# Reading attention scores two slots at a time, splitting the next stage's context from slot 6, and normalising rows on ScalarE in a fused decoder kernel

## The reference

```python
# first attention of layer 0: sign weights, 32 heads of 16, 8 key/value heads
q = x_n @ sign(Wq).T * scale_q     # k, v likewise; scale = mean |w| per output row
attn = softmax(q @ k.T / 4)        # per head, 64 x 64 scores
x = x + (attn @ v) @ sign(Wo).T * scale_o
# then: cross-attention with heads of 128, RMS-normed q and k; sparse feed-forward
# layer 1: attention with ALiBi and causal mask, cross-attention with key mask,
#          mixture of experts with a gate over 8 experts
```

## Time and profile before

| | |
|---|---|
| median of 3 runs | 2214.14 us (2213.44 to 2216.16) |
| the profiled execution's own time | 2213.81 us |
| its span, first to last instruction | 2212.0 us |
| mean granted TensorE clock | 0.99 of full |
| TensorE busy | 2118.3 us, 96% |
| VectorE, ScalarE, GpSimd busy | 61%, 46%, 41% |
| DMA | 82 MB, mean 37 GB/s |

### The profile page before, as it was taken

The page is one execution under the profiler, slowest core; times in us unless marked ns, Lnnn a source line. Parts: engine busy times, 40 slices in busy tenths (PEclk is TensorE's granted clock), DMA queues, the critical chain, the costliest instruction groups (busy, mean ns, idle before and its releaser), DMA issues. The chain is left out here.

```text
span 2212.0 us, 45005 instructions
## 1 busy us (share of the span) xinstructions
PE 2118.3 (96%) x18686; PEld 1718.5 (78%) x18686; DVE 1344.8 (61%) x2350; ACT 1028.0 (46%) x1754; POOL 902.6 (41%) x675
## 2 busy tenths in 40 slices
PE   6997999999999999999999999999998899999998
PEld 5665888888887888888888877888887677777766
DVE  6985544443334453444433558797785788888856
ACT  5774553545535455354543552111102667667632
POOL 2787241432414414143241345122122668778611
PEclk9998999999999999999999999999999899999999
DMA  4000111110112101111010123000002100100002
GB/s 168 2 21 21 48 33 55 39 47 32 40 39 77 58 21 39 39 39 58 21 40 36 44 66 98 1 0 0 0 1 76 31 7 21 50 27 11 2 1 77
DMA packets 23374, 82.06 MB, mean 37 GB/s; under 512 B 4112, under 2 KB 6288, under 8 KB 17040
## 3 DMA queue, kind: packets, MB, share of 16 engines
q1 hardware_dynamic: 23184, 79.33, 10.6%
HBM read 74.08 MB, written 4.19 MB: 35 GB/s over the span
## 5 line engine op out<-in xcount | busy, mean ns | idle before, releaser
L2644 PE MATMUL xat_TP<-shared_rounded 128*128 128x512 f32 x1024 | 321.6, 395 | 0.1
L2316 POOL TENSOR_TENSOR xat_T<-xat_T,xat_mask 128x512 f32<-128x512 f32 x64 | 82.1, 1295 | 479.3 <-DVE xat_T L2406 479.3
L104 PE MATMUL xat_G<-xat_xnT_hi,shared_rounded 128*128 128x512 f32 x768 | 244.5, 391 | 0.0
L2303 POOL TENSOR_TENSOR shared_rounded<-shared_landing,shared_rounded 128x2048 fp32r<-128x2048 f32 x39 | 179.5, 4609 | 152.4 <-ACT shared_rounded L2160 152.4
L2644 PEld LDWEIGHTS xat_TP<-shared_rounded 128*128 128x128 f32 x1024 | 188.3, 188 | 44.6 <-issue 6.2
L2644 PE MATMUL xat_TP<-shared_rounded,xat_oT_lo 128*128 128x512 f32 x512 | 199.6, 390 | 0.0
L2397 DVE RECIPROCAL xat_q_inv_rms<-xat_OT 128x16 f32<-128x16 f32 x32 | 8.3, 258 | 304.7 <-PE xat_OT L2569 304.7
L104 PE MATMUL ffn_H<-shared_rounded 128*128 128x448 f32 (+1 forms) x816 | 178.8, 368 | 3.7 <-DVE ffn_h_kept L1469 2.5
L1401 POOL TENSOR_TENSOR ffn_one_hot<-ffn_one_hot,ffn_block_rank 128x448 f32<-128x448 f32 x64 | 75.3, 1176 | 253.6 <-DVE ffn_one_hot L1450 253.6
L1377 ACT ACTIVATE shared_rounded<-ffn_TP 128x384 fp32r<-128x384 f32 x64 | 34.8, 544 | 293.4 <-PE ffn_Y L1526 246.7
L104 PEld LDWEIGHTS ffn_H<-shared_rounded 128*128 128x128 f32 x816 | 152.3, 188 | 20.8 <-DVE ffn_h_kept L1469 5.0
(11 more groups left out here) (363 smaller groups left out, 4959.5 us busy)
## 6 DMA issues: line engine op xcount, KB each, us to landing
shared_landing<-in_Cq_q SPq DMA_DIRECT2D x16, 1024.0 KB, 4.8
shared_landing<-in_Cq_o SPq DMA_DIRECT2D x16, 1024.0 KB, 4.8
shared_landing<-in_Cq_kv SPq DMA_DIRECT2D x8, 1024.0 KB, 8.2
shared_landing<-in_ctxT_paired SPq DMA_DIRECT2D x4, 1024.0 KB, 7.1
two_ctxT_raw<-in_ctxT SPq DMA_DIRECT2D x8, 512.0 KB, 4.0
shared_landing<-in_w1T SPq DMA_DIRECT2D x8, 448.0 KB, 3.7
shared_landing<-in_w SPq DMA_DIRECT2D x7, 512.0 KB, 3.7
out<-X SPq DMA_DIRECT2D x6, 512.0 KB, 3.0
```

What stands on the lines that cost most here:

```text
L104: last = eng.matmul(out, a, b, start=(n == 0), stop=(n == len(steps) - 1))
L2303: return eng.tensor_tensor(w[1][:, :, :], landed[:, :, :], w[0][:, :, :].bitcast(F32), ALU.subtract)
L2316: eng.tensor_tensor(T[:, n, :, :], T[:, n, :, :], mask[:, :].unsqueeze(1).to_broadcast([P, ROWS, SEQ]), ALU.add)\
L2644: last = eng.matmul(TP[m % 2][:, :], x, w, start=(n == 0), stop=(n == len(steps) - 1))
```

## The change

It has three parts. VectorE reads the scores of slots s and s+1 in the even slot s, from slot 2 on, in both uses of `small_attention`, and T's ring has 12 units in place of 8. In the last stage only the bias additions move; the maxima stay in their own slots. The early splits of the first attention begin at slot 6 (`NP - 2`) and end at slot 17. The first attention's rows of groups 2 and 3 are normalised on ScalarE, with VectorE's reciprocal and small operation ahead of the slot's maxima.

```diff
-    RING = 8
+    RING = 12
...
-            ln = LayerNorm(mem, X, ident, eps, by_tile=True, groups=NX, xn=xn, kept=lead["xnT"], stats=consts["stats"])
+            ln = LayerNorm(mem, X, ident, eps, by_tile=True, groups=NX, xn=xn, kept=lead["xnT"], stats=consts["stats"], on_act=True)
...
-            EARLY = {2 * NP + n: n for n in range(3 * KC)}
+            EARLY = {NP - 2 + n: n for n in range(3 * KC)}
...
-                for i in range(2, NG + 1 if pair else 0):
+                for i in range(2, NG + 1 if pair else NG):
                     for t in norm_slots(i).get(s, ()):
                         ln.scalar_xn(eng, i, t)
...
-                    for i in range(2, NG):
-                        for t in norm_slots(i).get(s, ()):
-                            ln.normed(eng, i, t)
...
-                for i in range(2, NG + 1 if pair else 0):
+                for i in range(2, NG + 1 if pair else NG):
                     if 0 in norm_slots(i).get(s, ()):
                         ln.vector_inverse(eng, i)
                 if s < LASTP:
-                    if sign:
-                        max_pair(s)
-                    else:
-                        take_scores(2 * s)
-                        take_scores(2 * s + 1)
-                if s < LASTP:
-                    if sign:
-                        shift_pair(s)
-                    else:
+                    for p in (s,) if s < 2 else (s, s + 1) if s % 2 == 0 else ():
+                        if sign:
+                            max_pair(p)
+                            shift_pair(p)
+                        else:
+                            take_scores(2 * p)
+                            take_scores(2 * p + 1)
+                    if not sign:
                         find_max(2 * s)
                         find_max(2 * s + 1)
...
-                        if sign and t == 0:
-                            ln.vector_inverse(eng, i)
-                        elif not sign and i > NG:
+                        if not sign and i > NG:
                             ln.vector_xn(eng, i, t)
```

## The result

The kernel after took 2228.52 us (median of 4 runs, 2228.06 to 2233.23) against 2213.79 before (4 runs, 2210.67 to 2216.16): ratio 1.0071, 95% interval 1.0057 to 1.0085, or +15.7 us (+12.6 to +18.8). The profiled executions are 2228.07 and 2213.81 us, +14.3; the forecast was +13.1 and 2227. The sum of the forecast was near, but several of its terms were not, and the experiments show which.

What follows compares the result with a forecast made beforehand. The prediction took TensorE, busy 96% of the span, as the bound. Terms of 9.7 us in the first attention and 3.4 in the last stage made +13.1 on 2213.81: 2227 us, range 2214 to 2237.

Steps and rivals of the forecast that it cites:

- Slot 3, first attention: Low halves come behind the moved VectorE pairs, so the key product starts later: +2.4 us, bounds 2.0 to 2.6.
- Statistics, slots 4, 5, 12, 13: First attention: normalisation variances come after ScalarE's table load wants them; +1.2 and +0.7 us, bounds 0 to 2.4 each.
- Group starts, first attention: Slots 8 to 11 and 16 to 19: y's product, then GpSimd's normalised unit, come later; twice 2.0, +4.0 us.
- Last group: First attention: moved pairs delay sum, reciprocal and GpSimd, so the transposition loops later; +1.2 us, bounds 0 and 2.4.
- Gain of early scores: First attention: TensorE waits less for freed scores; -0.2 us.
- Edit 2: Splits from slot 6: copies ahead of turned probabilities in slots 12 and 14; +0.4 us, bounds -0.5 and +1.0.
- Edit 3: Rows on ScalarE: delay in slots 6 to 8 covered by VectorE's four pairs, 0; uncovered, +1.9 us twice.
- Last stage: Later reads cost +1.2 us at slot 3, +1.0 over seven group boundaries, +1.2 at slots 62 and 63: +3.4.
- (a): Rival, 17%: only VectorE's order counts, ScalarE and GpSimd stay covered; +7.8 us, 2222 us.
- (b): Rival, 8%: faster; early-freed score banks, the first attention's last group closes up at full clock; 2207 us.
- (c): Rival, 8%: no change; half the faster rival's gain offsets slot 3, or TensorE catches up in later gaps; 2214 us.
- (d): Rival, 7%: a new loop in all even slots, sum and normalisation setting each pair, ScalarE uncovered; +20, 2234 us.

Runs made afterwards that it cites:

- e2: Kernel before with only the twelve early splits moved to slots 6 to 17, no early reading; timed +2.4 us (0.4 to 4.4).
- e4: Kernel before with splits in slots 6 to 17 and rows normalised on ScalarE, no early reading, ring of 8; timed +3.5 us, ratio 1.0016.
- e1: Kernel before with only the early reading of scores and the ring of 12, in both stages; timed +10.8 us (8.2 to 13.5).
- e3: Kernel before with only the first attention's eight later rows normalised on ScalarE instead of GpSimd; timed +3.1 us (1.1 to 4.9).
- edit 2: Second part of the change: the twelve early splits run in slots 6 to 17 instead of 16 to 27; alone against the kernel before, timed +2.4 us.
- e6: Kernel after, but the first two slots of every group read scores in their own slot, both stages; by timed ratio 5.3 us under the kernel after.
- edits 2 and 3: Second and third parts of the change: splits from slot 6, and rows normalised on ScalarE; together against the kernel before, timed +3.5 us.
- e7: Kernel after, but the first attention's last group (slots 24 to 31) reads each slot's scores in its own slot; timed ratio 1.0062.
- e8: Kernel after, but in the first attention's even slots VectorE makes the previous slot's sum and reciprocal between the two slots' reads; timed ratio 1.0065.
- e10: Kernel after with the ring of 8 in place of 12; timed ratio 1.0080.
- e12: Kernel after, but ScalarE normalises each group's third and fourth rows in slots 8 and 16, behind the first copy; no timed value given.
- e9: Kernel after, but early reading in the last stage alone, the first attention's order as before; timed ratio 1.0036.
- e5: Kernel after, but both stages read early only from slot 4 on; by trace 3.3 us less in the first attention, no timed value given.
- e11: Kernel after with no split in slots 8 and 16, these moved to 17 to 19; group starts unchanged at 2.0 us each, no timed value given.

## Why the prediction was right, and where it was not

- *Slot 3, first attention*, +2.4: the wait was 2.5, the term 3.4 in this pair of traces and 2.8 in the mean of all kernels. The mechanism was right. The forecast's upper bound of 2.6 left no room for slower TensorE behind the wait, which it thought of in the last stage only; most of the 1 us, though, is that the kernel before ran at a high clock there.
- *Statistics, slots 4, 5, 12, 13*, +1.9: measured 0 in slots 4 and 5; slots 12 to 15 show 0.7, but so do e2 and e4 (0.7, 0.85), which don't read early, and e1 and e3 don't (0.03 each), so it is edit 2's. The step that failed is the slack 60.24 - 59.00. The table load doesn't wait for the variances, only the root behind it does, and both come later by slot 3's 3.5. ScalarE and then VectorE in the kernel after:

```profile
63.79 1.28 ACT L219 ACT_TABLE_LOAD   x1
65.08 0.30 ACT L219 ACTIVATE gqa_ln_small<-gqa_ln_small,headmask_eps 128x4 f32<-128x4 f32 x1
```

```profile
64.68 0.28 DVE L187 BATCH_NORM_AGGREGATE gqa_ln_small<-stats 128x2 f32<-128x6 f32 x3
```

  The variances end at 64.96 and the root starts at 65.08: hidden behind the load, which was the forecast's lower bound.
- *Group starts, first attention*, +4.0: measured 3.99, by the steps given (y's product +2.4, the key's wait used up, then GpSimd with a subtraction ahead of unit 16). But the shares are other than the forecast's. It gave 0.9 of each 2.0 to VectorE's order, the rest to GpSimd behind it, and nothing to ScalarE's rows. By the runs the order is worth 0.7 (0.74 alone in e1 by slot 12, 0.7 less in e6), and 1.1 to 1.3 are there with edits 2 and 3 and no early reading at all (e4, e6). The two add up to the 2.07 of after by slot 12, though e4 waits for other things than after does.
- *Last group*, +1.2: right place and right loop (e7, e8), 3.2 in size. Each round cost 0.7 where 0.3 to 0.4 was forecast. The reading of the round left out what TensorE does after a wait of 2.1: its transposition takes 1.12, not 0.71, and 0.4 per round is just that. The forecast also stopped at slot 30, and 1.1 came behind it; e2, e3 and e4 show that too (1.1 to 1.4), and e1, e10 and e12, which do read early, only 0.2 to 0.3, so it goes with no edit. From slot 24 to the second attention together the kernels without this loop lie at -0.2 to +1.3.
- *Gain of early scores*, -0.2: TensorE's waits for scores fell by 0.8 in all, at places that the group starts counted. Nothing to see beyond.
- *Edit 2*, +0.4: alone 1.2 by the trace up to slot 30. The copies ahead of the turned probabilities came as forecast, +1.0 over slots 10 to 15 (+0.8 in after) and -0.3 from slot 20 to 22. Missed were the second group start, +1.7, and the last group, where leaving was to bring nothing and brought -1.6.
- *Edit 3*, 0 under cover: that holds (e12). Without cover it cost 0.75 at each group start alone (e3) and 1.27 with a split's copy beside it (e4), where the forecast's price was 1.9; the rest of e3's 2.7 stands behind slot 30, where its instructions are those of before. The three small operations delayed nothing that TensorE waited for, but they show the lock of which the forecast said that no row shows it. The Trainium skill ("SBUF — State Buffer", SBUF: two separate sides) says that of a VectorE operation with two SBUF inputs and a GpSimd one that reads SBUF the one that starts first holds the shared port for its whole instruction, and the other is blocked. The traces agree, for the case that GpSimd starts first. With GpSimd idle the small operation takes 0.16 us; beside GpSimd it ends when GpSimd's instruction ends. VectorE and GpSimd in the kernel after (a pair of normalisations is two instructions of 1.04 us, so their first ends at 67.48 and 111.23; VectorE's end at 67.50 and 111.25):

```profile
25.43 0.16 DVE L194 SCALAR_TENSOR_TENSOR gqa_ln_small<-gqa_ln_small 128x4 f32<-128x4 f32 x1
...
67.05 0.45 DVE L194 SCALAR_TENSOR_TENSOR gqa_ln_small<-gqa_ln_small 128x4 f32<-128x4 f32 x1
...
110.51 0.74 DVE L194 SCALAR_TENSOR_TENSOR gqa_ln_small<-gqa_ln_small 128x4 f32<-128x4 f32 x1
```

```profile
66.44 2.05 POOL L745 TENSOR_TENSOR gqa_T<-gqa_T,gqa_row_inv 128x512 f32<-128x512 f32 x2 [0.90 <-DVE gqa_row_inv L862]
...
110.19 2.04 POOL L745 TENSOR_TENSOR gqa_T<-gqa_T,gqa_row_inv 128x512 f32<-128x512 f32 x2
```

- *Last stage*, +3.4: 2.3 in the kernel after. Slot 3's wait grew by 0.93 (by 1.20 in e9 against e4), its slot by 0.5, under the lower bound of 0.9, since the product behind it took 0.6 less. Slots 4 to 7 cost 0.35, which the forecast had at nothing. The seven group starts cost 2.2 against 1.0; with early reading taken out of them it is 0.03 (e6), and seven of the eight other kernels that have it there show 2.1 to 2.2 (e10 5.4, with its wait for the ring). Most of it is in the groups that begin at slots 24, 32 and 48 (0.4, 0.65, 0.65) and near 0 at the others, where one size had been put on all. At slot 62 the wait grew by 0.9 as forecast, and then a product ran at the full clock (3.02 us in place of 4.53, behind the same wait of 2.65), which gave 1.5 back. The forecast had no way to this gain, so for it that is luck. Nor is it sure: seven of the ten kernels with early reading in this stage have the fast product, e5, e6 and e12 don't (4.34 to 4.60, and e6 lost 2.0 there), and none of the four without has it. What decides it no run shows.
- *Rivals*: (a) falls, since TensorE waits 9.0 us for GpSimd; (b) and (c) fall at the last group, though without early reading (b)'s gain of the clock is there, in e2, e4 and e9; (d) behind the group starts, where an even slot costs nothing more (+0.8 from slot 10 to 16, -0.3 from 18 to 24).

Measured, the first attention is 3.4 (slot 3) + 2.0 + 0.8 (slots 10 to 16) + 2.0 - 0.3 + 3.2 = 11.1, forecast 9.7; the last stage 2.3, forecast 3.4; and 0.8 lie outside both. So the direction and the places were understood, and that the total came within 1.2 us is luck: 1.9 for the statistics and 1.1 too much in the last stage stood against 1.0 at slot 3, 2.0 in the last group and the 0.8 outside.

## What to carry to other kernels

When work is read ahead on an in-order engine, the gain is the wait that its producer has for it (here 1.6 us), and the price is paid by everything that stood behind it in the queue: so look for what the bounding engine waits for at each place where a pipeline starts, and put the moved work behind that. Price two edits that feed the same wait together, and test them apart and together: at the second group start edits 2 and 3 covered each other (1.7 and 0.7 alone, 1.3 together), while the early reading came on top of both (0.7 and 1.1 to 1.3 alone, 2.0 together). And before a slower matmul is put down to the wait ahead of it, look at the matmul ahead of the wait, and at the same place in every other trace there is: two of the differences here (the 1 us at slot 3, the 1.6 us in e9 against e4) come for the most part from one execution with a high clock.

## What the runs showed of the hardware

*The clock at one place differs between executions.* Before the twelve matmuls of slot 62 in the last stage TensorE waits 2.65 us in every trace; they took 3.02 us in the kernel after, 4.53 before and 4.60 in e6. Those of slot 3 took 3.00 us in e4, 4.58 in e9 and 5.26 before. Behind a wait of 1.84 us in the first attention the four matmuls of a transposition took 0.65 before, 0.79 in e2, whose instructions are the same up to there, and 1.12 in e4. Busy time and granted clock, 45 to 60 us, of the kernel after:

```profile
45.00:60.00 15.00, 13.15 (x116) 10.57 (x120) 9.11 (x15) 7.20 (x13) 4.53 (x4) 0.71 0.00 1
```

and the same stretch of the kernel before:

```profile
45.00:60.00 15.00, 12.94 (x130) 10.08 (x131) 12.37 (x25) 9.11 (x17) 4.76 (x5) 0.89 0.01 1
```

The last column but two is the clock: TensorE is busy longer in the first and gets fewer matmuls through (116 against 130). In that stretch e2, e4 and e5, with the short wait too, had 0.80 to 0.82; e6 and e7, with the long one (4.23 us), 0.69 and 0.71, and e8, e10 and e11, with it as well, 0.77. So the longer wait goes with a lower clock, but it explains only a part of the step from 0.89 to 0.71. The clock has two levels, 1.2 and 2.4 GHz, and the moment at which it changes was worth 0.6 to 1.6 us at one place.

*A VectorE operation waited out the GpSimd instruction beside it.* The small VectorE operation shown above (four columns, two inputs in SBUF) occurs 187 times in the traces of all kernels. The 53 that start while GpSimd is idle take 0.16 us. The 134 that start while a GpSimd instruction runs take 0.45 to 1.02 us, and every one of them ends 0.01 to 0.02 us after that instruction does.
